# A two-layer audio tower with experts: 192 channels cut as 128 plus 64 rows instead of 96 plus 96, the qkv bias as a bfloat16 matmul of three rows, and a new order of the work in a round

## The reference

```python
h = tok(x)                                   # pairs of rows, softmax over the two, weighted sum -> 128 tokens
h = h + wkv_attention(layernorm(h))          # r, k, v: three 192x192 products; a recurrence over time; a 192x192 product
h = h + gelu(layernorm(h) @ W_in.T + b) @ W_out              # 192 -> 768 -> 192
hc = layernorm(h)
q = layernorm(hc @ Wq.T); k = layernorm(hc @ Wk.T + bk); v = hc @ Wv.T + bv
h = h + softmax_attention(q, k, v, heads=12) @ Wo.T + bo + hc
h = h + experts(layernorm(h))                # 8 experts of 192 -> 768 -> 192, the two best of each token
```

## Time and profile before

| | |
|---|---|
| median of 3 runs | 1989.87 us (1985.87 to 1995.31) |
| profiled execution | 1986.31 us |
| its span, first to last instruction | 1984.5 us |
| mean granted TensorE clock | 0.916 |
| PE, DVE, ACT, POOL busy | 1745.2, 1462.2, 1223.9, 782.6 us |

### The profile page before, as it was taken

The page is one execution under the profiler, slowest core; times in us unless marked ns, Lnnn a source line. Parts: engine busy times, 40 slices in busy tenths (PEclk is TensorE's granted clock), DMA queues, the critical chain, the costliest instruction groups (busy, mean ns, idle before and its releaser), DMA issues.

```text
span 1984.5 us, 33324 instructions
## 1 busy us (share of the span) xinstructions
PE 1745.2 (88%) x10605; PEld 1339.9 (68%) x10605; DVE 1462.2 (74%) x2753; ACT 1223.9 (62%) x3205; POOL 782.6 (39%) x756
## 2 busy tenths in 40 slices
PE   2478899999999999998999998873899999999996
PEld 1344675666666666665665656652799999999996
DVE  3676687787787787887886864332789998989994
ACT  1234677677677676776776766651666666656662
POOL 1001123233233133143143142222477777777775
PEclk8679899999999999999999988775899999999998
DMA  3000011011011011011011010063576776767660
GB/s 92 24 17 8 1 33 55 4 52 54 0 54 54 0 54 54 0 54 54 0 54 54 0 39 31 23 203 100 154 178 148 171 164 168 164 147 185 151 159 1
DMA packets 121093, 146.38 MB, mean 74 GB/s; under 512 B 20755, under 2 KB 99718, under 8 KB 121030
## 3 DMA queue, kind: packets, MB, share of 16 engines
q1 hardware_dynamic: 88608, 113.83, 19.0%
q0 software_dynamic: 28608, 29.93, 8.2%
q10 hardware_dynamic: 3814, 1.83, 0.4%
HBM read 93.84 MB, written 48.14 MB: 72 GB/s over the span
## 4 chain that ended last, share of the span: by engine, by line
PE 66%; DVE 14%; ACT 7%; issue 6%; DMA 4%; POOL 1%; SPq 1%; ACTq 0%; POOLq 0%; DVEq 0%
PE ps L778 13%; PE ps L476 10%; PE ps L791 9%; PE ps L559 6%; PE ps L627 4%; PE ps L793 4%; ACT probs L916 4%; DMA xt<-in_x 3%; PE ps L643 3%; PE ps L656 3%; PE ps L485 3%; PE ps L585 2%; PE ps L551 2%; PE ps L759 2%; DVE q_s L1306 1%
## 5 line engine op out<-in xcount | busy, mean ns | idle before, releaser
L916 ACT ACTIVATE probs<-ps,nmax 128x128 f32<-128x128 f32 x768 | 270.2, 375 | 136.8 <-DVE nmax L1377 136.7
L1174 POOL DMA_INDIRECT out<-ey,etoken x156 | 280.3, 1797 | 149.9 <-DMA out<-ey,etoken 60.6
L791 PE MATMUL ps<-w_hl,h_hi 128*128 128x384 f32 x936 | 273.0, 363 | 3.1 <-DVE ey L1613 3.1
L1051 ACT ACTIVATE h_full<-ps,eb 128x512 f32<-128x512 f32 x234 | 167.8, 717 | 174.0 <-PE ps L778 174.0
L793 PE MATMUL ps<-w_hl,h_lo 128*128 128x192 f32 x936 | 235.1, 251 | 0.0
L1377 DVE TENSOR_REDUCE nmax<-ps 128x6 f32<-128x768 f32 x128 | 120.3, 951 | 124.6 <-PE ps L627 124.5
L551 PE MATMUL ps<-hTB,w_up 96*128 96x512 f32 x384 | 184.4, 620 | 4.4 <-ACT hid L897 3.2
L793 PEld LDWEIGHTS ps<-w_hl,h_lo 128*128 128x128 f32 x936 | 179.7, 192 | 0.0
L791 PEld LDWEIGHTS ps<-w_hl,h_hi 128*128 128x128 f32 x936 | 176.7, 189 | 3.4 <-issue 3.3
L1164 POOL TENSOR_TENSOR w_lo<-w_raw,w_hi 128x1536 fp32r<-128x1536 f32 x39 | 157.6, 4040 | 36.6 <-ACT w_hi L1032 36.6
L1142 POOL DMA_INDIRECT expert_rows_in<-rowR,slot_i x128 | 152.4, 1191 | 48.3 <-issue 46.3
(11 more groups left out here) (228 smaller groups left out, 3909.1 us busy)
## 6 DMA issues: line engine op xcount, KB each, us to landing
w_raw<-in_L_ffn_w SPq DMA_DIRECT2D x39, 576.0 KB, 4.6
ex<-expert_rows_in SPq DMA_DIRECT2D x39, 528.0 KB, 5.4
w_raw<-in_L_ffn_w SPq DMA_DIRECT2D x39, 384.0 KB, 5.4
w_raw<-in_L_ffn_w SPq DMA_DIRECT2D x78, 192.0 KB, 5.7
xt<-in_x SPq DMA_DIRECT2D x16, 768.0 KB, 5.5
expert_rows_in<-xt SPq DMA_DIRECT2D x17, 528.0 KB
hA_kept<-hA SPq DMA_DIRECT2D x16, 384.0 KB, 5.9
out<-resC SPq DMA_DIRECT2D x16, 384.0 KB, 3.4
```

The lines of the kernel that those rows point to most:

```text
L791: nc.tensor.matmul(ps[:, 4 + s, 0:2 * C], h_hi[b][:, m, q], w2_hl[b][:, m, :], start=(m == 0), stop=False)
L916: last = nc.scalar.activation(probs[:, t % 2, HJ * c + j, :], ps[:, 4 + j, c * P:(c + 1) * P], ACT.Exp, bias=nmax[:, t, j, c:c + 1], accum ...
L1051: nc.scalar.activation(h_full[:, m, :], ps[:, m % 4, :], ACT.Gelu, bias=eb1[u][:, m:m + 1])
L1174: nc.gpsimd.indirect_dma_start(total, bass.IndirectOffsetOnAxis(ap=etoken[u][:, s:s + 1], axis=0), ey[b][:, s, :], None, bounds_check=NB * ...
```

## The change

The channels are cut as chunk 0 = channels 0 to 127 and chunk 1 = channels 64 to 191, each on all 128 rows, so that channels 64 to 127 stand in both. All elementwise work of VectorE and ScalarE on channel-major tiles runs on 128 rows instead of 96, over the same number of columns. The result of chunk m takes its own chunk whole (one matmul of 128 rows) and from the other chunk only the 64 channels that it lacks. These two 64-row matmuls lie on different halves of the array (`rest(0)` is rows 64 to 127, `rest(1)` rows 0 to 63) and write to different banks. The bias is added by two bfloat16 matmuls of three rows (a float32 number as the sum of three bfloat16 numbers, prepared at the start). The q, k and v columns are regrouped so that each of two banks gets 288 columns.

```diff
+            return [(w[:, 0], ap[0:P]), (w[:, 1], ap[CL:C])]
...
+            def rest(n):
+                return slice(CL * (1 - n), CL * (1 - n) + CL)
+
             def channels_out(bank, w, rhs):
-
                 for m in range(KC):
-                    for k in range(KC):
-                        last = nc.tensor.matmul(ps[0:CC, bank + m, :], w[:, k, m * CC:(m + 1) * CC],
-                                                rhs[:, k * N:(k + 1) * N], start=(k == 0), stop=(k == KC - 1))
+                    nc.tensor.matmul(ps[:, bank + m, :], w[:, m, m * CL:m * CL + P], rhs[:, m * N:(m + 1) * N],
+                                     start=True, stop=False)
+                for m in range(KC):
+                    k = 1 - m
+                    last = nc.tensor.matmul(ps[:, bank + m, :], w[rest(m), k, m * CL:m * CL + P],
+                                            rhs[rest(m), k * N:(k + 1) * N], start=False, stop=True)
                 return last
...
+                for t in range(2):
+                    o = [ps[:, bank + n, t * C:(t + 1) * C] for n in range(2)]
+                    at = [(2 * n + t) * T for n in range(2)]
+                    for n in range(2):
+                        nc.tensor.matmul(o[n], xT[:, n * N + at[n]:n * N + at[n] + T], w[:, n, :],
+                                         start=True, stop=False)
+                    for n in range(2):
+                        k = 1 - n
+                        last = nc.tensor.matmul(o[n], xT[rest(n), k * N + at[n]:k * N + at[n] + T],
+                                                w[rest(n), k, :], start=False, stop=True)
...
+                    half, o = C + C // 2, [ps[:, bank + n, 0:C + C // 2] for n in range(2)]
+                    for n in range(2):
+                        nc.tensor.matmul(o[n], hTC[:, n, t * T:(t + 1) * T], w_qkv[:, n, n, :],
+                                         start=True, stop=False)
+                    nc.tensor.matmul(ps[:, bank, C:half], ones_bf[0:3, :], b_qkv[:, 0:C // 2],
+                                     start=False, stop=False)
+                    nc.tensor.matmul(o[1], ones_bf[0:3, :], b_qkv[:, C // 2:2 * C], start=False, stop=False)
+                    for n in range(2):
+                        last = nc.tensor.matmul(o[n], hTC[rest(n), 1 - n, t * T:(t + 1) * T],
+                                                w_qkv[rest(n), 1 - n, n, :], start=False, stop=True)
...
+                    for k, rows in enumerate((slice(0, P), rest(0))):
+                        last = nc.tensor.matmul(ps[:, 6, t * E:(t + 1) * E], hTC[rows, k, t * T:(t + 1) * T],
+                                                w_router[rows, k, :], start=(k == 0), stop=(k == KC - 1))
...
-            init = Chain(dve, S["d_init"], 2)
+            init = Chain(dve, S["d_init"], 8)
```

The rows are alike; what moved is the group: the store is now that of group `i - 3`, and `load_x(3)` and `keep_h(2)` have moved ahead of the loop. On VectorE `a_delta` goes from behind `a_scan_p` to in front of `c_max(gr, 3, 0)`, and the last `c_attn_add` goes from in front of `a_scan_p` to behind it:

```diff
-                if gr is not None: c_attn_add(gr, 3)
-                if ga is not None: a_scan_p(ga)
-                if gn is not None: a_delta(gn)
                 if ga is not None: a_scan_q(ga)
...
+                if gr is not None: c_values(gr, 1)
+                if gn is not None: a_delta(gn)
+                if gr is not None: c_max(gr, 3, 0)
...
+                if ga is not None: a_scan_p(ga)
                 if gr is not None: c_attn_add(gr, 3)
```

More of the change, by code:

```diff
@@ L64, in build_tower @@
     CH = 128
-    CL = C - CH
     INFO = 8
@@ L363, in _ @@
                 sp.dma_start(dst, src).then_inc(S["weights_in"], 16)
-            assert len(loads) == SP_LOADS
+            half = C // 2
+            loads += [
+                (chan[0:half, :, 0], a["L0_chan"][:, :, 0]),
+                (chan[half:P, :, 0], a["L0_chan"][0:P - half, :, 1]),
+                (chan[0:half - CL, :, 1], a["L0_chan"][CL:half, :, 0]),
+                (chan[half - CL:P, :, 1], a["L0_chan"][:, :, 1]),
+            ]
+            for dst, src in loads[-4:]:
+                sp.dma_start(dst, src, allow_slow_non_contiguous=True).then_inc(S["weights_in"], 16)
+            assert len(loads) == SP_LOADS, len(loads)
             def load_x(g):
@@ L662, in r_logits @@
                 for t in range(G):
-                    for k in range(KC):
-                        last = nc.tensor.matmul(ps[:, 6, t * E:(t + 1) * E], hTC[0:CC, k, t * T:(t + 1) * T],
-                                                w_router[:, k, :], start=(k == 0), stop=(k == KC - 1))
+                    for k, rows in enumerate((slice(0, P), rest(0))):
+                        last = nc.tensor.matmul(ps[:, 6, t * E:(t + 1) * E], hTC[rows, k, t * T:(t + 1) * T],
+                                                w_router[rows, k, :], start=(k == 0), stop=(k == KC - 1))
                 last.then_inc(S["logits_psum"], 1)
@@ L722, in round_ @@
-                if gc is not None: c_values(gc, 0, gb)
-                if gc is not None: c_scores(gc, 2, 0)
-                if gc is not None: c_scores(gc, 2, 1)
-                if gc is not None: c_queries(gc, 3, gb)
-                if gn is not None: a_r(gn)
-                if gc is not None: c_values(gc, 1, gb)
-                if gc is not None: c_scores(gc, 3, 0)
-                if gc is not None: c_project(gc, 0)
-                if gc is not None: c_scores(gc, 3, 1)
-                if gn is not None: a_k(gn)
@@ L732, in round_ @@
-                if gc is not None: c_project(gc, 1)
-                if gc is not None: c_values(gc, 2, gb)
+                if gb is not None: b_mlp_up(gb, 2)
+                if gb is not None: b_mlp_up(gb, 3)
             pe.wait_ge(S["weights_in"], 16 * N_LOADS)
```

313 lines of the change are left out of this document (163 added, 150 removed).

## The result

The changed kernel takes 1917.35 us (median of four runs, 1913.04 to 1921.70), the kernel before 1987.87 beside it. The ratio is 0.9639, with a 95% interval of 0.9604 to 0.9675. The prediction was 1912 us; the time is the one of its likeliest case.

A forecast was written before the change was run, and what follows sets the result against it. TensorE was taken to bound the kernel, busy 69.81 of a 75.09 us round. From 1986.3 us, 78 for 14 rounds and 1 for the last interval come off, 5 for the start is added: 1912 us, range 1885 to 1930.

The forecast's parts named there:

- likeliest case: The forecast itself, chance 0.55: 1912 us, with rounds of 69.5 us.
- The round: Steady round of 66.0 work, 2.3 waits and 1.2 clock: 69.5 us, 5.6 less, 78 us over 14 rounds.
- Packing is nearly a wash: TensorE's matmuls: passes save 7.8 us a round, row changes cost 7.0, so work falls 0.8 to 0.9.
- The changes of rows: TensorE switching between 128, 64 and 32 rows: 0.2 us each, 0.1 in r_logits, together 7.0 us a round.
- (a) to (e): New order's effect on TensorE's waits: a_delta, exponentials, oT, routing covered; vpad stays; 2.3 us a round left.
- The three waits named: TensorE's waits for a_delta (1.5 us), the exponentials (0.9) and oT (0.6), forecast to go.
- Step (a): SyncE's xt load no longer waits for a current group's store; TensorE's 1.5 us wait for a_delta goes.
- (b): a_r fills the 0.9 us wait ahead of the scores' second half; its own lateness leaves 0.6.
- (f): TensorE's clock: one of two waits ahead of its fall goes, so 1.2 us a round lost instead of 2.9.
- The start: Ahead of the rounds: six more DMAs on ScalarE's queue cost 3 us, the bias split some 2; together 5.
- The last interval: The shorter interval after the 14 rounds, with fewer stages, 60.5 us before: gives 1 us.
- The slower rival: The 64-row pairs take turns, so savings vanish and switches stay: round 76.9 us, 2017 us; chance 0.08.

The follow-up runs named there:

- the order alone: The new order of all engines and SyncE's queue, with the kernel before's matmuls and layouts: 1908.81 us, ratio 0.9585; again on the slower chip 1948.84 us, 0.9601.
- pairs in turn: Changed kernel with both 64-row matmuls of each pair on the same rows, so they can't run side by side: 2079.25 us, ratio 1.0438.
- store late: Kernel before with SyncE issuing the xt load ahead of the store of group i-3, not behind that of i-2: 1979.92 us, ratio 0.9953.
- three moves: Store late plus a_r between the halves of the third scores and a_delta ahead of a_scan_p, against the kernel before: 1988.66 us, ratio 1.0000.
- each piece alone: Packed matmuls in the old order, each b_mlp_up piece as one 128-row and one 64-row matmul announced at its own end: 2137.03 us, ratio 1.0724.

## Why the prediction was right, and where its steps were off

**The round.** 69.5 was forecast and 69.53 came, partly by errors that cancel. The saving was smaller than the 5.6 us forecast, since the round before is 74.65 us on average and 75.09 in my sample: 14 rounds gave 71.5 us and not 78. I started from one sample round, and counted 2.9 us lost to the clock from two groups of matmuls in it; the whole stretch of the earlier trace rows has 6.83 us busy at 0.51 and loses 3.3. Over 14 rounds the loss is 4.1, and the work 65.0 instead of 66.9 (the sample has 454 matmul records, the average round 447). The three parts moved like this: work −1.7 (forecast −0.9), idle time −1.9 (forecast −3.0), clock −1.5 (forecast −1.7). In absolute terms 66.0 of work, 2.3 of waits and 1.2 for the clock were forecast, and 63.3, 3.6 and 2.6 came: the work was taken 2.7 us too high, waits and clock 2.7 too low. That these cancel is luck.

**Packing is nearly a wash: right in the time, not in the way there.** Pairs run side by side (7.8 us more work when they don't, against 8.5). The changes of rows don't cost all that the passes save: work falls by 1.4 to 1.6 us against the order alone, and idle time and the clock take it back, which the sum had not. The Trainium skill, "TensorEngine Tiling (Array Packing)", says under Key Properties that a change of mode drains the engine. The trace agrees in so far as every change costs time: a `tokens_out` takes 2.74 us where twelve passes of 0.163 are 1.96, 0.2 for each of four changes, and the third piece of `c_qkv` gave 0.2 for each as well. Taken out, others gave 0.1 to 0.15. `r_logits` was sized right: 0.8 us for its eight changes, and the same stretch takes 0.8 to 0.9 us more than the earlier trace rows have. The term that was mis-sized is `c_qkv`: 0.6 us for its three changes and 2.2 us a piece were forecast, and the pieces take 2.01 to 2.12, which is most of the 0.8 us by which the work fell further. By itself, packing makes the kernel 0.6% slower in the new order (0.9662 / 0.9601) and 3.0% slower in the old one. The second I had not costed: an announcement that comes at the end of a pair is a change of order by itself.

**(a) to (e), the waits: each named one as forecast, their sum too low, and wrong in reasoning.** The three waits named are gone, that for `vpad` stayed at its 1.1, and `a_r` waits 0.8 for its mix (0.6 forecast). But two new ones, 0.7 for `qT` and 0.6 for `hid`, bring the round from 546.06 to 3.2 us and the average to 3.6, where 2.3 was forecast. Nor are the waits independent terms. Step (a) by itself sheds its wait and brings half a per cent; with the moves for (b) beside it nothing is left of that. Only the whole list brings 4.8 us a round.

**(f), the clock.** The loss was to fall by 1.7 and fell by 1.5. That it would be low behind the scores in some rounds and not in all came true: in the round from 546.06 it is 0.50 from 568.60 to 572.00, behind the waits for `vpad` and for `a_r`'s mix, and the first four passes of `a_r` take 3.47 us instead of the 1.98 of the next round. What (f) had not is a second place, where no wait of TensorE stands ahead: `r_logits` and the `b_mlp_up` behind it (0.50 from 677.85 to 681.25). Three rounds in a row, from 546.06, 617.01 and 686.46, have both places, the second alone, and none, and take 70.95, 69.45 and 67.82 us. Each stretch is 3.4 us long, half of the one before.

**The start.** 5 us were forecast; the rounds' first work begins 3.6 later. ScalarE's queue ends its last weight load at 14.73 instead of 11.00, yet VectorE begins only 1.3 us later, and the split of the bias takes another 2.4 (19.45 to 21.83):

```profile
14.73 0.35 ACTq L1050 DMA_DIRECT2D b_raw<-in_L_attn_bv  x1
...
18.08 0.76 DVE L1244 COPY decay<-chan 128x512 f32<-128x512 f32 x2 [11.02 <-issue]
...
19.45 0.34 DVE L1254 CAST b_part<-b_raw 3x384 bf16<-3x384 f32 x1
...
21.48 0.35 DVE L1260 CAST b_qkv<-b_raw 3x384 bf16<-3x384 f32 x1
...
28.06 1.02 ACT L887 ACTIVATE wkv<-ps 128x1024 f32<-128x1024 f32 x1 [3.77 <-DMA b_columns<-hid]
```

In the kernel before, the last row's counterpart stands at 24.45.

**What I missed.** The rounds in which the pipeline fills: from there to the first keys the changed kernel gains 12 us (8.6 + 3.6). The order alone has its first keys at 195.8, so this too is the order's. The last interval was to give 1 us and costs 3.8 (62.3 us with the order alone, 64.3 with the packing as well, against 60.5), and the part behind it costs 3.0. So the sum holds because the fill makes up for what the rounds (6.5 us) and the end fall short: that too is luck.

**The slower rival** (pairs in turn, 2017 us) was tried as an experiment and gives 2079: its round was 76.9 us and is 80.09, since the sum gave nothing to the clock, which takes 6.2; its work, 74.6 in the sum, is 71.0, and its idle time 2.9 against 2.3.

What stays open: which moves of the order carry the gain, beyond those tried, which carry half a per cent (store late) and nothing (three moves); and what sets TensorE's clock. With each piece alone it costs three times what the kernel before loses, at less idle time.

## What to carry to other kernels

Split a round into idle time, work at full clock and what the clock takes, from one row of stretches; the first tells of waits, the second of the matmuls alone, and a change that moves one into another brings nothing. Packing two 64-row matmuls paid here only once few changes of row mode came with it (0.5% slower with 39 changes a round, 2.3% faster with 21, both against the order alone), so pad short matmuls with zeros to the mode that stands around them, and put what shares a mode back to back. Where a change makes two results ready together, look at what is queued behind the reader of the first.

## What the runs showed of the hardware that I had not expected

- The stretches at the lower clock in the rows above and in the earlier trace rows last 3.40, 6.9 and 10.2 us. One of 3.4 us at half the clock costs 1.7 us, and that is the step between the rounds of the changed kernel (67.8, 69.5 and 71.0 us from keys to keys).
- A wait taken from TensorE can come back as lower clock: in full in the profiled run of store late (idle −1.0, clock +1.5, round the same), in part in its other runs.
- The four passes of a 64-row pair over 512 columns take 1.13 us on different rows, 1.98 on the same.
- Padding with zeros costs nothing: the router's 16 passes take 1.95 us on 128 rows, 1.92 on 96, and 2.72 with every second one on 64.
- The same kernels are 2% slower on one chip (2027 against 1990 us), in the rounds with more lost to the clock (4.0 against 2.6 us for the changed kernel) and more idle time (4.7 against 3.6), while the experts take the same time (596 against 598 us). Why is open.
